# Rank counts of a mixture-of-experts router: six fp16 matmuls, or a running sum on VectorE and two fp32 matmuls

## The reference

```
logits = xf @ gate_w.T
sc = softmax(logits)
_, idx = top_k(sc, 2)
...
h = silu(xf @ w1.T) * (xf @ w3.T)
y = sum over the two experts of weight * (h @ w2.T)
```

## Time and profile before

| what | value |
|---|---|
| median of three runs | 1555.55 us (1553.91 to 1556.95) |
| profiled execution: time | 1556.95 us |
| profiled execution: span from the first to the last instruction | 1555.4 us |
| TensorE busy | 1457.8 us, 94% of the span |
| VectorE busy | 1255.0 us, 81% |
| ScalarE busy | 880.7 us, 57% |
| GpSimd busy | 320.0 us, 21% |
| granted TensorE clock, mean | 0.964 of full |

### The profile page before, as it was taken

How to read it: one execution, slowest core, us unless ns; L and a number is a source line. 1 busy time by engine, 2 the same in 40 slices (tenths; PEclk the granted TensorE clock), 3 DMA queues, 4 the chain that set the end, 5 groups by cost and what they waited for, 6 DMA issues and landing times.

```text
span 1555.4 us, 38010 instructions
## 1 busy us (share of the span) xinstructions
PE 1457.8 (94%) x15152; PEld 1281.3 (82%) x15152; DVE 1255.0 (81%) x2182; ACT 880.7 (57%) x1275; POOL 320.0 (21%) x251
## 2 busy tenths in 40 slices
PE   7999899969999999999999899858999999999996
PEld 6777688866678999999997644448899999999995
DVE  8999777765666788888888789877978887888795
ACT  4114387765435677777773245545666666666651
POOL 1000156640300000000004067743600000000050
PEclk9999999988999999999999789869999999999999
DMA  7550000014756788988873011029888888888884
GB/s 192 151 135 24 11 1 2 2 59 146 211 180 225 270 290 308 291 304 298 306 285 109 18 34 33 18 106 339 281 291 304 285 301 283 307 286 302 290 270 108
DMA packets 55560, 297.68 MB, mean 191 GB/s; under 512 B 14063, under 2 KB 14319, under 8 KB 32433
## 3 DMA queue, kind: packets, MB, share of 16 engines
q1 hardware_dynamic: 41761, 263.23, 49.6%
q0 software_dynamic: 13712, 33.26, 7.9%
HBM read 264.07 MB, written 32.34 MB: 191 GB/s over the span
## 4 chain that ended last, share of the span: by engine, by line
PE 74%; DVE 17%; ACT 3%; issue 2%; POOL 2%; DMA 1%; DVEq 0%; POOLq 0%; ACTq 0%; SPq 0%
PE ps L779 14%; PE ps L758 10%; PE ps L760 10%; PE ps L762 10%; PE ps L2405 5%; PE ps L2388 5%; DVE wl L1464 3%; PE ps L2325 3%; PE ps L2517 3%; DVE wl L1465 3%; PE ps L2311 2%; PE ps L2200 2%; POOL wl L1027 2%; PE ps L791 2%; DVE wl L635 1%
## 5 line engine op out<-in xcount | busy, mean ns | idle before, releaser
L758 PE MATMUL ps<-big,wh 128*128 128x176 f16 x2160 | 496.1, 240 | 8.6 <-DVE wl L635 6.4
L762 PE MATMUL ps<-big,wl 128*128 128x176 f16 x2160 | 496.2, 238 | 0.0
L760 PE MATMUL ps<-big,wh 128*128 128x176 f16 x2160 | 496.1, 238 | 0.0
L779 PE MATMUL ps<-big,wh 128*128 128x176 f16 x2160 | 262.7, 238 | 1.0 <-DVE big L669 1.0
L779 PE MATMUL ps<-big,wl 128*128 128x176 f16 x1080 | 248.9, 239 | 0.0
L635 DVE SCALAR_TENSOR_TENSOR wl<-ext,wh 128x2304 f16<-128x2304 f32 x90 | 229.6, 2552 | 2.0 <-issue 1.8
L635 DVE SCALAR_TENSOR_TENSOR wl<-raw,wh 128x2304 f16<-128x2304 f32 x90 | 229.5, 2550 | 0.0
L554 ACT ACTIVATE wh<-raw 128x2304 f16<-128x2304 f32 x90 | 190.4, 2117 | 55.9 <-PE ps L779 55.4
L758 PEld LDWEIGHTS ps<-big,wh 128*128 128x128 f16 x2160 | 208.6, 97 | 12.5 <-DVE wl L635 6.0
L554 ACT ACTIVATE wh<-ext 128x2304 f16<-128x2304 f32 x90 | 190.5, 2117 | 47.9 <-PE ps L779 33.7
L760 PEld LDWEIGHTS ps<-big,wh 128*128 128x128 f16 x2160 | 211.2, 98 | 0.2
(11 more groups left out here) (373 smaller groups left out, 2811.5 us busy)
## 6 DMA issues: line engine op xcount, KB each, us to landing
raw<-in_units SPq DMA_DIRECT2D x54, 1152.0 KB
ext<-in_units SPq DMA_DIRECT2D x54, 1152.0 KB, 5.6
raw<-in_units SPq DMA_DIRECT2D x36, 1153.0 KB, 5.8
ext<-in_units SPq DMA_DIRECT2D x36, 1153.0 KB, 5.8
raw<-in_units_s SPq DMA_DIRECT2D x16, 769.0 KB, 4.3
ext<-in_units_s SPq DMA_DIRECT2D x16, 769.0 KB, 4.6
x_slots<-logs SPq DMA_DIRECT2D x1, 8976.0 KB
big<-x_slots POOLq DMA_DIRECT2D x17, 528.0 KB, 8.4
```

Source lines behind the costliest of these rows:

```text
L758: nc.tensor.matmul(o, wh[:, u % RING, w_], x_, start=c == 0 and m == 0, stop=False, skip_group_check=True)
L760: nc.tensor.matmul(o, wh[:, u % RING, w_], xTl[:, c, 0:ph.n], start=False, stop=False, skip_group_check=True)
L762: ins = nc.tensor.matmul(o, wl[:, u % RING, w_], x_, start=False, stop=c == KC - 1, skip_group_check=True)
L779: ins = nc.tensor.matmul(o, l_[:, u % RING, w_], r_, start=first and k == 0 and c % 2 == 0, stop=last and k == 2, skip_group_check=True)
```

## The change

The fp16 array and the fp16 copies of the two matrices go. VectorE now keeps the sum of the two one-hot arrays in fp32 (`sel`) and makes of it a running sum over the tiles in 48 elements (`held`): group 0 is zero, group t + 1 is group t plus tile t. TensorE multiplies `held` by ones in one fp32 matmul of 48 columns, which gives the rows of all earlier tiles for each group and the counts in group 5, and adds the triangular product of `sel` in one fp32 matmul of 40 columns.

```diff
-        tri16 = sb("tri16", [P, P], F16)
-        ones16 = sb("ones16", [P, P], F16)
...
-            nc.vector.tensor_copy(tri16[:, :], tri[:, :])
-            nc.vector.tensor_copy(ones16[:, :], ones[0:P, 0:P])
...
+            held = flat(sm[:, 8:10], (NT + 1) * NE).rearrange("p (t e) -> p t e", e=NE)
...
             def held_by_tile():
 
-                nc.vector.tensor_tensor(sel16, oh[:, 0], oh[:, 1], ALU.add).then_inc(s_rd, 1)
+                nc.vector.memset(held[:, 0, :], 0.0)
+                step(nc.vector.tensor_tensor(sel, oh[:, 0], oh[:, 1], ALU.add))
+                step(nc.vector.tensor_copy(held[:, 1, :], sel[:, 0, :]))
+                for t in range(1, NT):
+                    ins = nc.vector.tensor_tensor(held[:, t + 1, :], held[:, t, :], sel[:, t, :], ALU.add)
+                    if t < NT - 1:
+                        step(ins)
+                ins.then_inc(s_rd, 1)
...
                 pe.wait_ge(s_rd, layer + 1)
                 o = bank(7)[0:P, 128:128 + (NT + 1) * NE]
-                nc.tensor.matmul(o[:, 0:NT * NE], tri16[:, :], sel16.rearrange("p t e -> p (t e)"), start=True,
-                                 stop=False, skip_group_check=True)
-                for t in range(NT):
-                    ins = nc.tensor.matmul(o[:, (t + 1) * NE:].rearrange("p (t e) -> p t e", e=NE), ones16[:, :],
-                                           sel16[:, t:t + 1, :].to_broadcast([P, NT - t, NE]), start=False,
-                                           stop=t == NT - 1, skip_group_check=True)
-                ins.then_inc(s_rk, 1)
+                held = sm[:, 8:10].rearrange("p a t e -> p (a t e)")[:, 0:(NT + 1) * NE]
+                nc.tensor.matmul(o, ones[0:P, 0:P], held, start=True, stop=False, skip_group_check=True)
+                nc.tensor.matmul(o[:, 0:NT * NE], tri[:, :], sm[:, 4, :, :].rearrange("p t e -> p (t e)"), start=False,
+                                 stop=True, skip_group_check=True).then_inc(s_rk, 1)
```

More of the change, by code:

```diff
@@ L315, in residual_bank @@
             return bank((6, 4, 6, 4, 4)[t], 2)[0:P, 0:D]
-        sel16 = sm[:, 4].rearrange("p t e -> p (t e)").bitcast(F16)[:, 0:NT * NE].rearrange("p (t e) -> p t e", t=NT)
         def z_turned(t):
@@ L1744, in _ @@
             flat = lambda a, n: a.rearrange("p a t e -> p (a t e)")[:, 0:n]
-            lgs, eq, oh, lg2 = sm[:, 0], sm[:, 1], sm[:, 2:4], sm[:, 5]
+            lgs, eq, oh, sel, lg2 = sm[:, 0], sm[:, 1], sm[:, 2:4], sm[:, 4], sm[:, 5]
             slot0, slot, prod, rev = sm[:, 6], sm[:, 7], sm[:, 10:12], cst8[:, 0]
+            held = flat(sm[:, 8:10], (NT + 1) * NE).rearrange("p (t e) -> p t e", e=NE)
             more = flat(prod, 3 * NE).rearrange("p (e k) -> p e k", k=3)
```

## The result

The changed kernel took 1565.78 us (median of four executions, 1565.06 to 1567.43) where the kernel before took 1555.4 us (four executions, 1553.91 to 1556.95): a ratio of 1.0065, with a 95% interval of 1.0046 to 1.0085. The forecast was 1557.0 us and its range ended at 1559.6. Three of the four executions of the kernel before were on record before the prediction, and the fourth came with the result; of the changed kernel the first session holds 29 executions in all. Most of this difference did not return: in three later sessions, each on another chip with both kernels executed in turn, the change cost 2.6 us (95%: 1.6 to 3.7; 36 executions of the changed kernel, 104 of the kernel before), and the kernel before took 1561.2 us in the mean, not 1555.4. Two later executions, at 2521 and 2179 us with a mean granted clock of 0.55 and 0.64, are left out of all these numbers.

The account below looks back on a forecast made before the run. TensorE was taken to bound the kernel (74% of the chain), with a serial VectorE and TensorE ladder in layer 1's routing. 1.07 + 0.24 + 0.10 = 1.4 us on the median 1555.55 gave 1557.0 us; range 1554.8 to 1559.6.

Parts of the forecast that it names:

- VectorE, layer 1: Layer 1 routing: five dependent small steps of 0.20 us plus a memset of 0.07, 1.07 us later.
- TensorE, layer 1: Layer 1 ranks: four fp32 records at the lower clock take 1.09 us against 0.85 for six fp16 matmuls, +0.24.
- TensorE, layer 0: Ranks in layer 0's shared-expert stream: four fp32 records, 0.46 us against about 0.36, +0.10.
- VectorE, layer 0: Layer 0's shared expert: the same +1.07 us, hidden by 3.01 us of VectorE idle time.
- the casts: Two removed casts at the start, 0.22 us each: gain 0, because VectorE then waits for TensorE anyway.
- What is late behind the ladder: Layer 1 slots, placement, pass table and weight transfer follow the ranks in the same order, so all move together.
- ladder: Layer 1 routing: serial small VectorE steps, then TensorE ranks, VectorE and gathering matmuls; nothing beside it, so time counts in full.
- rival C: Layer 1: the first pass's weight transfer is bound elsewhere and absorbs the delay, leaving 0.1 us, 1555.7 us; chance 0.14.
- Rivals A and B: TensorE's clock behind layer 1's ranks: unchanged return point, +0.75, 1556.3 us (0.14); or later return, +3.65, 1559.2 us (0.10).
- How the numbers follow: Chances and range for the whole kernel: forecast 0.58, within 0.2% 0.83; a median wanders by about 1 us.
- the base of the sum: Whole kernel: the median of the three runs shown, 1555.55 us, to which the 1.4 us were added.

Follow-up runs that it names:

- The 25 additions: 25 dependent 8-element VectorE additions behind layer 1's selection sum, in the kernel before: +8.9 us; with GpSimd's last gathers also held back: +1.8 us.
- e8: Kernel before with 25 dependent 8-element VectorE additions behind layer 1's selection sum: +8.9 us (6.7 to 11.0) against the kernel before.
- e15: Kernel before with 25 small additions in layer 1 and GpSimd's last gathers held back: +1.8 us (-0.7 to 4.2) against the kernel before.
- the hold: GpSimd's last gathers wait for ScalarE's casts of further last-pass weights; in the kernel before, -2.1 and -4.2 us, together -3.1 us (-4.6 to -1.7).
- the padded kernel: Changed kernel with the two 16-bit matrices still allocated but unused, keeping the old addresses: +1.5 us (-0.1 to 3.0) against the kernel before.

## Why the prediction was wrong, by its own steps

- *VectorE, layer 1*: 1.07 us forecast, 1.01 measured (1.26 - 0.25). The memset ran beside the sum and cost nothing; five steps of 0.20 are as forecast.
- *TensorE, layer 1*: +0.24 forecast, +0.24 measured (1.09 against 0.85). By the four passes of the Trainium skill ("FP8 and Floating Point Precision", TensorE Precision Notes) the prediction had estimated +0.16 instead of +0.24; the trace shows two records for each matmul, and +0.24. Two records don't speak against four passes: a record of line 2459 takes 0.248 us for 132 columns at 1.2 GHz, which is 298 cycles, over twice its columns.
- *TensorE, layer 0*: +0.10 forecast, +0.03 to +0.06 measured.
- *VectorE, layer 0* and *the casts*: hidden, as forecast. Idle time fell to 1.99 us (1.9 forecast) and rose to 1.00 us (0.9 to 1.2 forecast).
- *What is late behind the ladder*: held, but this pair of profiles can't show it. ScalarE's wait for the first weights of layer 1 is again 6.7 us. Waits of ScalarE in that stretch, changed kernel (before: the earlier trace rows):

```profile
ACT wh L550 <- DMA ext<-in_units: 6.7, 1, 6.7
```

That they are equal is chance: the wait is 5.5 to 9.1 us over the 18 profiles. From the selection's sum to the cast that waited it is 25.1 us before, 25.7 after, so the weights came only 0.6 us later for a ladder 1.25 us longer; the five profiles with layer 1 unchanged range from 23.9 to 26.5. The 25 additions stand clear of that range, with 30.4 us (e8) and 31.1 (e15). The cast of the kernel before, on the timeline:

```profile
1063.82 2.12 ACT L554 ACTIVATE wh<-ext 128x2304 f16<-128x2304 f32 x1 [6.67 <-DMA ext<-in_units]
```

And of e8, whose sum of the selection starts at 1044.42:

```profile
1074.79 2.12 ACT L554 ACTIVATE wh<-ext 128x2304 f16<-128x2304 f32 x1 [8.31 <-DMA ext<-in_units]
```

So the transfer moves with the ladder, and rival C falls.

- *Rivals A and B, the clock's return behind the ladder*: neither. Changed kernel, the first gathering matmul on the timeline:

```profile
1052.13 1.21 PE L2575 MATMUL ps<-mask,logs 125*128 125x176 f16 x7 [5.50 <-DVE mask L1835]
```

and the stretch of 2 us in which the clock returns:

```profile
1056.00:1058.00 2.00, 2.00 (x26) 2.00 (x25) 1.24 (x6) 0.56 (x2) 1.60 (x2) 0.89 0.49 103
```

0.89 puts the return at about 1056.4, 4.3 us behind that matmul; before it was 4.4. The clock did matter, but in graph attention, 30 us ahead of the changed ladder, where the prediction had not looked.
- *How the numbers follow*: this is the step that failed, together with the base of the sum. "The three runs shown spread over 3.0 us, so a median wanders by about 1 us" took three executions of one session as samples of the kernel's whole spread, and the sum was added to their median. The base was 5.7 us too low (1561.1 - 1555.4). Only one of those executions was profiled, and it was lucky twice: it has the shortest graph attention of the 18 profiles (134.56 us, with four others within 0.2 us, where the ten with nothing changed ahead of it have a mean of 137.6) and the shortest last pass of the fourteen without the hold (31.71, where their mean is 34.3). These two make 5.6 us. The changed kernel's first session was high by 1.8 us: 29 executions there have a mean of 1565.7, the 36 later ones 1563.9. With the 2.6 us of the change that makes the 10 us.

The effect itself, 1.4 us forecast, lies just below the bounds of the pooled 2.6 us (1.6 to 3.7), and at the lower bound of the 2.3 us (1.4 to 3.3) that include the padded kernel. Its mechanism, the ladder, was right; the time it was added to was not. The ladder's 1.25 us and layer 0's 0.05 are what the traces show of it. Another 1.3 us (0.3 to 2.4) has no place that I could show: more than one to one behind the ladder (slope 1.6) would give 0.8 of it, and the addresses (-0.9 to 2.0) could be part of it.

Why four executions of the kernel before all came within 1556.95 us is open too. Of the 129 later ones 12 did, so four independent draws would do so once in some 13,000 times; something was common to them that the later sessions lack. The changed kernel's first 29 executions were off too, but to the other side, 1.8 us above its later ones. The chip of the first session isn't on record, and no later session showed the like, so a chip on which the change costs more is not excluded.

## What to carry to other kernels

Where a serial chain of small VectorE steps stands alone, count its steps: each 8-element step is 0.20 us, and four fewer TensorE instructions don't buy five of them back. Before you add a small term to a median, ask how far executions of different sessions lie apart, and compare the two kernels in turn on one chip. In a difference of two profiles, first set aside stretches ahead of the change: what moved there isn't the edit.

## What the runs showed of the hardware

- The same code and data took 134.6 to 142.4 us in graph attention, with 31 to 45 us of it spent at TensorE's lower clock level (correlation 0.92). The Trainium skill ("TensorE: Matmul & The Clock Gate", What's actually happening) has the point where the clock comes back vary from run to run. The traces agree, and show that the points where it falls vary too (991.7 us before, 1001.8 after in the same code); the stage's 7.9 us between shortest and longest are 0.5% of the kernel.
- The last weight transfer, of 1.15 MB, took 13.1 to 19.2 us while GpSimd gathered rows by indirect DMAs, and 11.2 to 13.1 us with the gathers held back by 5 to 9 us; the median transfer takes 5.7 us. Other weight transfers were under way beside it in both cases.
- Four fp32 records of 40 and 48 columns took 1.09 us up to their reader at the lower clock when TensorE had been idle, and 0.36 us within a busy stream at the full one (1.00 granted from 390 to 392).
